# Products of weights for a cross-attention moved from a stage of their own into the recurrent layer's stage of a two-layer decoder kernel

## The reference, cut to what matters

```
x = x + rwkv(ln(x))            # recurrent layer: sigmoid(r) * (decayed sums), then Wo
x = x + xattn(ln(x), context)  # 16 heads, latent keys and values of width 64
x = x + experts8(ln(x)); x = x + gqa(ln(x)); x = x + xattn2(ln(x), context); x = x + experts16(ln(x))
```

```
k, v, r = x @ Wk.T, x @ Wv.T, x @ Wr.T ; w = exp(clip(k)) ; w[:, 0] *= exp(time_first)
num_t = decay * num + w_t * v_t ; den_t = decay * den + w_t        # per channel, over 256 steps
out   = (sigmoid(r) * num / (den + 1e-6)) @ Wo.T

q_big  = rope(einsum(x @ Wq.T, w_kc_q))      # 16 heads x 192
scores = (q_big @ W_qr) . (rope(ctx) @ W_kr) ; attn = softmax(scores)
out    = ((attn @ rope(ctx)) @ w_kc_kv.T) @ Wo.T
```

## Time and profile before

| | |
|---|---|
| time before, median of 3 runs | 1548.04 us |
| lowest and highest of the runs | 1537.82 and 1548.26 us |
| the profiled execution: its own time | 1536.56 us |
| its span (first to last instruction) | 1534.8 us |
| PE busy, share of the span | 1386.6 us, 90% |
| DVE busy | 910.4 us, 59% |
| ACT busy | 641.4 us, 42% |
| POOL busy | 860.8 us, 56% |
| mean granted TensorE clock | 0.947 of full speed |

### The profile page before, as it was taken

The page is one execution under the profiler, slowest core; times in us unless marked ns, Lnnn a source line. Parts: engine busy times, 40 slices in busy tenths (PEclk is TensorE's granted clock), DMA queues, the critical chain, the costliest instruction groups (busy, mean ns, idle before and its releaser), DMA issues.

```text
span 1534.8 us, 21060 instructions
## 1 busy us (share of the span) xinstructions
PE 1386.6 (90%) x7568; PEld 904.0 (59%) x7568; DVE 910.4 (59%) x1615; ACT 641.4 (42%) x1630; POOL 860.8 (56%) x766
## 2 busy tenths in 40 slices
PE   6579997999999999999998567998999988889998
PEld 3466554555555555555557553445777844478887
DVE  6855666566666566666633438996663146646555
ACT  2320112444444444444440324887662247724332
POOL 4415000788888898888890435886442025515554
PEclk9778998899999999999999688998999999979999
DMA  9200111000000000000007320000000041000000
GB/s 263 91 1 14 35 35 35 8 8 8 8 12 8 8 11 7 8 8 11 8 4 251 97 68 9 0 1 1 1 1 25 1 126 63 2 0 1 1 1 28
DMA packets 53375, 48.64 MB, mean 32 GB/s; under 512 B 18048, under 2 KB 49688, under 8 KB 52760
## 3 DMA queue, kind: packets, MB, share of 16 engines
q1 hardware_dynamic: 52504, 45.20, 10.8%
q0 software_dynamic: 768, 2.10, 0.4%
HBM read 34.18 MB, written 4.72 MB: 25 GB/s over the span
## 4 chain that ended last, share of the span: by engine, by line
PE 76%; DVE 10%; ACT 6%; issue 3%; POOL 2%; DMA 1%; SPq 0%; DVEq 0%; POOLq 0%; ACTq 0%
PE PS L435 71%; PE PS L443 4%; ACT s_sc L1120 2%; DVE s_mx L1536 1%; ACT a_m L1086 1%; DVE pm L1357 1%; DVE r_den L1279 1%; DVE PS L1380 1%; POOL a_m L1728 1%; ACT s_pt L944 1%; DVE HN L1229 1%; PE PS L578 1%; POOL a_m L1722 1%; ACT a_sq L1095 1%; ACT QKT L944 1%
## 5 line engine op out<-in xcount | busy, mean ns | idle before, releaser
L1670 POOL TENSOR_TENSOR PWS<-PWS 128x1024 f32<-128x1024 f32 x160 | 379.8, 2373 | 79.8 <-ACT PWS L1026 63.7
L1026 ACT ACTIVATE PWS<-PS 128x512 f32<-128x512 f32 (+1 forms) x416 | 227.8, 595 | 270.0 <-PE PS L435 258.3
L1357 DVE TENSOR_REDUCE pm<-PS 128x2 f32<-128x1024 f32 x192 | 227.4, 1221 | 86.9 <-PE PS L435 86.3
L435 PE MATMUL PS<-PWS,KVR 128*64 128x256 f32 (+1 forms) x1664 | 207.4, 387 | 0.0
L435 PE MATMUL PS<-QALL,KH 128*128 128x512 f32 (+1 forms) x416 | 187.9, 452 | 1.5 <-ACT PWS L1026 1.5
L435 PE MATMUL PS<-QM,KL 68*128 68x512 f32 (+1 forms) x416 | 166.6, 400 | 0.0
L1743 POOL TENSOR_SCALAR s_sc<-s_sc,s_ri 128x128 f32<-128x128 f32 (+1 forms) x256 | 103.9, 425 | 104.0 <-DVE s_ri L1543 104.0
L435 PEld LDWEIGHTS PS<-PWS,KVR 128*64 128x64 f32 (+1 forms) x1664 | 109.8, 137 | 86.4 <-issue 34.7
L1120 ACT ACTIVATE s_sc<-PS,s_nb 128x128 f32<-128x128 f32 (+1 forms) x256 | 104.4, 427 | 58.6 <-DVE s_nb L1539 58.6
L435 PEld LDWEIGHTS PS<-QALL,KH 128*128 128x128 f32 (+1 forms) x416 | 77.7, 187 | 73.0 <-issue 35.6
L1536 DVE TENSOR_REDUCE s_mx<-PS 128x2 f32<-128x512 f32 (+2 forms) x112 | 65.7, 611 | 52.8 <-PE PS L435 52.8
(11 more groups left out here) (279 smaller groups left out, 2854.5 us busy)
## 6 DMA issues: line engine op xcount, KB each, us to landing
QALL<-qlo SPq DMA_DIRECT2D x32, 128.0 KB, 2.4
QM<-QALL SPq DMA_DIRECT2D x64, 64.0 KB, 2.0
f_w<-in_L_ffn_w_dram SPq DMA_DIRECT2D x2, 2048.0 KB
a_nat<-in_L_attn_w_qkv_dram SPq DMA_DIRECT2D x1, 3072.0 KB, 21.5
x_wq<-in_L_xattn_Wq_dram SPq DMA_DIRECT2D x1, 2048.0 KB, 9.3
x_wo<-in_L_xattn_Wo_dram SPq DMA_DIRECT2D x2, 1024.0 KB, 6.7
a_wo<-in_L_attn_w_o_dram SPq DMA_DIRECT2D x1, 2048.0 KB, 21.1
m_wd<-in_L_ffn_Wd_dram SPq DMA_DIRECT2D x1, 2048.0 KB, 8.3
```

The source lines that it names most:

```text
L435: return nc.tensor.matmul(o, a, b, start=start, stop=stop, **kw)
L1026: nc.scalar.activation(PW[c][0:rows, j * HALF:(j + 1) * HALF], PS[0:rows, k % 2 * 512:(k % 2 + 1) * 512], ACT.Exp).then_inc(p_ready, 1)
L1357: ins = V.tensor_reduce(pm[u % 2][:, :, i // 3, i % 3], src, AX, ALU.max)
L1670: G.tensor_tensor(ACC[:, :], PW[0][:, :] if i == 0 else ACC[:, :], PW[i + 1][:, :], ALU.add).then_inc(acc_step, 1)
```

## The change

The work of stage 1 is put into stage 0, between W1 and the wait for `rw_ready`; `ended(eng, 0)` goes, and the later barriers and SP's waits on them count one less. So that this can be done:

- ACT and POOL wait for a new semaphore `scans_done` before they write buffers that lie where the scans' inputs were. DVE gives it after the last scan, on a memset of 128 x 1.
- Buffers move: WqrS to 40960 (over r_decay), x_woT to 145152 (over x_wq), W2 to 104480 (over x_wo0 and r_nat), and WkrT becomes WkrP at 161664 (over x_wqr).
- ACT empties "xwo" and "w2" in place of DVE: the eight "w2" jobs with one copy of 128 x 512 each.
- WkrP holds for each pair of heads three blocks of 64 columns, of which the middle one is zero. With it the two half-height products have 128 moving columns rather than 64 and write the zero quarters themselves. The memset of W2 goes; POOL sets the middle blocks of WkrP (64 x 512) instead.
- POOL makes both strided copies of 64 x 1536 for WqrS.
- `split(0)` on POOL waits for the last "w1" job.

```diff
-        WqrS = at("WqrS", 12288, [D, H * QW])
-        WkrT = at("WkrT", 24576, [D, H * D])
-        x_woT = at("x_woT", 28672, [P, H, C])
+        WqrS = at("WqrS", 40960, [D, H * QW])
+        WkrP = at("WkrP", 161664, [D, PAIRS, 3, D])
+        x_woT = at("x_woT", 145152, [P, H, C])
-        W2 = at("W2", 112672, [P, PAIRS, 2, 256])
+        W2 = at("W2", 104480, [P, PAIRS, 2, 256])
...
             eng.drain().then_inc(phase_ended, 1)
-            eng.wait_ge(phase_ended, 4 * (n + 1))
+            eng.wait_ge(phase_ended, 4 * n)
...                                                     # PE, after the 16 "w1" jobs
-            pe.wait_ge(rw_ready, KC)
-            for t in range(NT):
-                out_product(("ro", t), [(r_num[:, ct, t * P:(t + 1) * P], r_wt[:, 3, ct, :]) for ct in range(KC)])
-            turn_x(1)
-            ended(pe, 0)
             pe.wait_ge(xattn_loaded, 16 * 4)
             for g in range(6):
                 turn(("wqr", g), "act", ...)
             for g in range(2):
                 turn(("wkr", g), "act", ...)
             for g in range(8):
-                turn(("xwo", g), "dve", ...)
+                turn(("xwo", g), "act", ...)
...                                                     # the 4 "u" jobs, unchanged
             pe.wait_ge(*banks.emptied(("wkr", 1)))
             pe.wait_ge(wqr_shift, 2)
+            pe.wait_ge(wkr_padded, 1)
             for p in range(PAIRS):
-                ps = begin(("w2", p), "dve")
+                ps = begin(("w2", p), "act")
                 for c, w in enumerate((WqrT, WqrS)):
-                    A = WkrT[:, 2 * p * D:(2 * p + 1) * D]
-                    A2 = WkrT[:, (2 * p + 1) * D:(2 * p + 2) * D]
+                    A = WkrP[:, p, :, :].rearrange("r k i -> r (k i)")
                     o, g = 256 * c, 3 * p * P
-                    mm(ps[:, o:o + 64], w[:, g:g + P], A)
-                    mm(ps[0:64, o + 64:o + 128], w[:, g + P:g + P + 64], A)
-                    mm(ps[64:128, o + 128:o + 192], w[:, g + P + 64:g + 2 * P], A2)
-                    last = mm(ps[:, o + 192:o + 256], w[:, g + 2 * P:g + 3 * P], A2)
+                    mm(ps[:, o:o + 64], w[:, g:g + P], A[:, 0:64])
+                    mm(ps[0:64, o + 64:o + 192], w[:, g + P:g + P + 64], A[:, 0:128])
+                    mm(ps[64:128, o + 64:o + 192], w[:, g + P + 64:g + 2 * P], A[:, 64:192])
+                    last = mm(ps[:, o + 192:o + 256], w[:, g + 2 * P:g + 3 * P], A[:, 128:192])
                 last.then_inc(filled, 1)
+            pe.wait_ge(rw_ready, KC)
+            for t in range(NT):
+                out_product(("ro", t), ...)
+            turn_x(1)
             ended(pe, 1)
...                                                     # ACT, after its 16 "w1" copies
+            act.wait_ge(scans_done, 1)
+            ...                                         # copies: 6 wqr, 2 wkr, 8 xwo, 4 u, 8 w2
             for g in range(2):
                 deviations(1, g)
...
-            nc.scalar.activation(*wqr_half(1), ACT.Copy).then_inc(wqr_shift, 1)
...                                                     # DVE
+                if ct == KC - 1:
+                    V.memset(pool_tick[:, 0:1], 0.0).then_inc(scans_done, 1)
...
-            for g in range(8):
-                copy_out(("xwo", g), x_woT[:, 2 * g:2 * g + 2, :])
-            V.tensor_copy(*wqr_half(0)).then_inc(wqr_shift, 1)
-            ...                                         # and four copies for each of 8 "w2" jobs
...                                                     # POOL, after kv_roped
-            ended(pool, 0)
-            G.memset(W2[:, :, :, :], 0.0).then_inc(w2_cleared, 1)
+            pool.wait_ge(scans_done, 1)
+            pool.wait_ge(*banks.emptied(("wqr", 5)))
+            for i in range(2):
+                G.tensor_copy(*wqr_half(i)).then_inc(wqr_shift, 1)
+            G.memset(WkrP[:, :, 1, :], 0.0).then_inc(wkr_padded, 1)
...
+            pool.wait_ge(*banks.emptied(("w1", H - 1)))
             split(0)
             ended(pool, 1)
```

More of the change, by code:

```diff
@@ L317, in decoder @@
         kv_roped = sem("kv_roped")
-        w2_cleared = sem("folded_weights_cleared")
+        wkr_padded = sem("key_weights_padded")
+        scans_done = sem("decayed_sums_ready")
         wqr_shift = sem("wqr_shifted")
@@ L515, in _ @@
             for g in range(8):
-                turn(("xwo", g), "dve", [x_wo[ot][:, h * P:(h + 1) * P] for h in (2 * g, 2 * g + 1) for ot in range(KC)])
+                turn(("xwo", g), "act", [x_wo[ot][:, h * P:(h + 1) * P] for h in (2 * g, 2 * g + 1) for ot in range(KC)])
             pe.wait_ge(kckv_loaded, 16)
@@ L527, in _ @@
             pe.wait_ge(wqr_shift, 2)
+            pe.wait_ge(wkr_padded, 1)
             for p in range(PAIRS):
-                ps = begin(("w2", p), "dve")
+                ps = begin(("w2", p), "act")
                 for c, w in enumerate((WqrT, WqrS)):
-                    A = WkrT[:, 2 * p * D:(2 * p + 1) * D]
-                    A2 = WkrT[:, (2 * p + 1) * D:(2 * p + 2) * D]
+                    A = WkrP[:, p, :, :].rearrange("r k i -> r (k i)")
                     o, g = 256 * c, 3 * p * P
-                    mm(ps[:, o:o + 64], w[:, g:g + P], A)
-                    mm(ps[0:64, o + 64:o + 128], w[:, g + P:g + P + 64], A)
-                    mm(ps[64:128, o + 128:o + 192], w[:, g + P + 64:g + 2 * P], A2)
-                    last = mm(ps[:, o + 192:o + 256], w[:, g + 2 * P:g + 3 * P], A2)
+                    mm(ps[:, o:o + 64], w[:, g:g + P], A[:, 0:64])
+                    mm(ps[0:64, o + 64:o + 192], w[:, g + P:g + P + 64], A[:, 0:128])
+                    mm(ps[64:128, o + 64:o + 192], w[:, g + P + 64:g + 2 * P], A[:, 64:192])
+                    last = mm(ps[:, o + 192:o + 256], w[:, g + 2 * P:g + 3 * P], A[:, 128:192])
                 last.then_inc(filled, 1)
+            pe.wait_ge(rw_ready, KC)
+            for t in range(NT):
+                out_product(("ro", t), [(r_num[:, ct, t * P:(t + 1) * P], r_wt[:, 3, ct, :]) for ct in range(KC)])
+            turn_x(1)
             ended(pe, 1)
@@ L982, in _ @@
                          lambda ps: ps[:, 0:KC * QW].rearrange("p (k q) -> p k q", k=KC))
+            act.wait_ge(scans_done, 1)
+            for g in range(6):
+                copy_out(("wqr", g), WqrT[:, g * HALF:(g + 1) * HALF], lambda ps: ps[0:D, :])
+            for g in range(2):
+                copy_out(("wkr", g), WkrP[:, 4 * g:4 * g + 4, 0:3:2, :],
+                         lambda ps: ps[0:D, :].rearrange("r (p s i) -> r p s i", p=4, s=2))
+            for g in range(8):
+                copy_out(("xwo", g), x_woT[:, 2 * g:2 * g + 2, :])
+            for g in range(4):
+                copy_out(("u", g), U[:, 2 * g:2 * g + 2, :])
+            for p in range(PAIRS):
+                copy_out(("w2", p), W2[:, p, :, :])
             for g in range(2):
@@ L1291, in _ @@
                     V.tensor_tensor(z_HTl[:, g, kc, :], ps, z_HTh[:, g, kc, :].bitcast(F32), ALU.subtract).then_inc(emptied["dve"], 1)
-            ended(dve, 0)
-            for g in range(8):
-                copy_out(("xwo", g), x_woT[:, 2 * g:2 * g + 2, :])
-            dve.wait_ge(*banks.emptied(("wqr", 5)))
-            V.tensor_copy(*wqr_half(0)).then_inc(wqr_shift, 1)
[L1299 to L1307, removed]
             ended(dve, 1)
@@ L1821, in _ @@
                 sp.wait_ge(q_moved[s], 32 * PAIRS)
-            sp.wait_ge(phase_ended, 4 * 3)
+            sp.wait_ge(phase_ended, 4 * 2)
             for u in range(UNITS):
@@ L1829, in _ @@
                                  QALL[h * D:(h + 1) * D, p, b, h, :].bitcast(F32)).then_inc(qh_moved[u % 2], 16)
-            sp.wait_ge(phase_ended, 4 * 4)
+            sp.wait_ge(phase_ended, 4 * 3)
             sp.dma_start(g_nat[:, :], L0_ffn_gate_weight).then_inc(moe0_loaded, 16)
@@ L1837, in _ @@
             sp.dma_start(a_wo[:, :, :], L1_attn_w_o.rearrange("(o p) k -> p o k", p=P)).then_inc(gqa_loaded, 16)
-            sp.wait_ge(phase_ended, 4 * 5)
+            sp.wait_ge(phase_ended, 4 * 4)
             sp.dma_start(a_cos[:, :, :], cos1_c).then_inc(gqa_bcast, 16)
@@ L1852, in _ @@
                              f_y[:, e % 3, :].rearrange("p (i c) -> p i c", i=2)).then_inc(res_sent[e % 3], 16)
-            sp.wait_ge(phase_ended, 4 * 6)
+            sp.wait_ge(phase_ended, 4 * 5)
             sp.dma_start(s_mask[:, :], mask_c).then_inc(masks_loaded, 16)
@@ L1861, in _ @@
             sp.dma_start(y_hm[:, :], hmask_c).then_inc(lat_loaded, 16)
-            sp.wait_ge(phase_ended, 4 * 8)
+            sp.wait_ge(phase_ended, 4 * 7)
             sp.dma_start(m_rw[:, :], L1_ffn_router_w).then_inc(moe1_loaded, 16)
@@ L1875, in _ @@
             sp.dma_start(m_wd[:, E1:E1X, :], L1_ffn_Sd[0].rearrange("(s i) c -> i s c", i=P)).then_inc(moe1_loaded, 16)
-            sp.wait_ge(phase_ended, 4 * 10)
+            sp.wait_ge(phase_ended, 4 * 9)
             for t in range(NT):
```

## The result

| | before | after |
|---|---|---|
| median of the runs (4 each) | 1548.15 us | 1526.03 us |
| lowest to highest | 1537.82 to 1549.62 us | 1524.66 to 1528.07 us |
| ratio | | 0.9872, 95% interval 0.9827 to 0.9917 |
| profiled execution, its span | 1536.56, 1534.8 us | 1528.07, 1525.9 us |
| first z product | 121.34 us | 104.39 us |

The changed kernel is faster by 1.3%. The medians are 22.1 us apart and the two profiled spans 8.9; the stretch that was changed became 17.0 us shorter (121.34 - 104.39).

A forecast was written before the change was run, and what follows sets the result against it. PE idled from 50.7 to 68.71 us behind DVE's reciprocals, then stage 1 took 34.8 us on PE. Moving it gave 26, taken as 25: 1511.6 from the profiled execution, 1523 from the median; predicted 1516, range 1508 to 1534.

The forecast's parts named there:

- rival 2: PE from U on: half clock all the way through U, W2 and output products; 9 us less; chance 0.06.
- the low level: Whole time: the profiled execution of before, 1536.6 us, next to the lowest run and 11.5 us under the median.
- Turns and U: Before W2: ACT's 16 bank copies, 8.8 us together, set U's start at 60.4; U takes 3.6 us, ending at 64.0.
- POOL: Ahead of W2: two strided copies at 1.6 us each and a 0.4 us memset, done at 58.5, hidden; cost 0.
- W2's columns: W2's half-height products: 128 moving columns for 64 add 0.11 us a group at full clock, 0.21 at half.
- W2's clock: W2 on PE: full clock held through 16 groups at 0.95, 15.2 us, ending at 79.2; 26.5 us at half.
- rival 1: W2: clock falls as before, 22.3 us, and output products start at half clock; 17 us less; chance 0.22.
- Output products to the barrier: After W2: 17.8 us before, 1.9 less at full clock, so 15.9 us, ending at 95.1.
- rival 3: Turns before U: they do not hold the clock, U starts 1 us later; about 23 us less; chance 0.06.
- Nothing after the start of the z products is altered: 1413.5 us that I leave as they are: From the first z product, 121.34 us before, to the end: 1413.5 us taken as unchanged.
- the sum of 1511.6: Whole time against the profiled execution: 1536.6 - 25 us.

The follow-up runs named there:

- pool_more: The changed kernel with POOL making each of its two 64x1536 copies four times over; first z product at 115.0 us, 10.6 us later.
- batched: The changed kernel with the four full-height products of both groups before the four half-height ones in each W2 job; median 1524.57 us, ratio 0.9837 to before.
- rowpair: The changed kernel with heads 8 to 15 in partitions 64 to 127, two pairs of heads at once in W2; median 1510.0 us, ratio 0.9764 to before.
- w2_twice: The kernel `rowpair` with each W2 product made twice into the same place; W2 from 63.3 to 76.4 us, first z product at 92.6 us.
- cols64: The changed kernel with 64 moving columns in W2's half-height products and its zero quarters left unset; 1528.0 us in one run.
- gap2: The changed kernel with W2 ordered as in `batched` and the last two W2 jobs between the halves of `turn_x(1)`; 1519.63 us, ratio 0.9829 to before.
- w2_late: The changed kernel with the W2 jobs behind the output products and the turns of the normalised x; 1538.5 us in one run.

## Why the prediction was right, and where it was not

- **Direction and size**: 1516 was predicted, within 1508 to 1534, and 1526.03 measured. The median fell by 22.1 us where 25 was forecast. That the two lie so close is in part luck: up to z only 17.0 us came of the 25, and the rest is from the later part, of which the prediction said that it stays. Nor does the range tell one mechanism from another: it was said to leave out rival 2, but from the low level rival 2 gives 1536.6 - 9 = 1527.6, inside it.
- **Turns and U**: U at 60.4 forecast, 58.83 measured. The copies took 0.50 us each (4.01 for eight), not 0.56. ACT was free at 58.74 and x_kckv landed at 58.37: two limits nearly level, of which I had named one. U took 3.6 us.
- **POOL**: 1.43 us a copy against 1.6, done at 57.8, hidden. `pool_more` bears the slack out.
- **W2's columns**: 0.11 and 0.21 us a group forecast, 0.10 and 0.22 measured.
- **W2's clock, the step that failed**: "16 * 0.95 = 15.2 us at full". The clock fell as in the kernel before, and W2 took 23.4 us. This is rival 1, whose 17 us less to z is what came (17.0), with parts that were off and cancelled: U began 1.6 us earlier than forecast, W2 took 1.1 more than the 22.3 of that rival, and the output products 0.7 more than 17.8. I gave it 0.22, although the row of before was the only evidence and spoke for it. The argument against it, more columns in nearly the same time, carried nothing: `batched` raised the density further and the clock fell sooner. What held it in `rowpair` and `w2_twice` was a second set of products in the other half of the rows.
- **Output products to the barrier**: 18.5 us (85.88 to 104.39), where 17.8 belongs to a start at half clock.
- **Turns and the clock**: rival 3 fell. 50.20 to 57.30 holds turns and is at 1.00, which again goes against what the Trainium skill says in "TensorE: Matmul & The Clock Gate", Part 4: PE-mode transpose, that turns do not bring the full clock.
- **"Nothing after the start of the z products is altered: 1413.5 us that I leave as they are"**: the instructions are the same, the time is not. It was 1413.5 to 1423.9 in three executions of one kernel. Against the profiled execution the sum of 1511.6 missed 1528.07 by 16.5 us: 8 in the early part (z forecast at 96.3) and 8 in the later one. Against the median, 1523 missed by 3, although the early part was off by the same 8 us: the later part made up for most of it.
- Of the 22.1 us between the medians, 17.0 to 18.2 are shown in the early part. The other 4 to 5 belong to executions without a trace; that they are shorter falls of the clock is argued only.

## What to carry to other kernels

Moving work into an engine's hole gives at most the smaller of hole and work, less what the moved work loses or plus what it gains in its new place (W2 took 19.4 us before and 23.4 after): read which row says at what clock it ran, and price it so until another row says otherwise. When small products with K = 64 follow each other on one half of the rows, look for a second set to put into the other half before looking at their order; it took W2 from 23.4 to 6.6 us. Take the trace of before more than once when the runs show two levels, and cut it at the first instruction that the change leaves alone: the second part tells how large a difference is no difference.

## What the runs showed of the hardware that was not expected

- TensorE, busy without a stop, went from 2.4 to 1.2 GHz within 2.8 to 5.7 us of products with K = 64 on one half of the rows, in every form that had them at full clock at the start (the kernel before, the changed one, `cols64`, `batched`, `gap2`). With the same products in both halves, two at a time, it stayed at 2.4 GHz for 13.1 us.
- Once down, such products do not bring it back: 26.7 us at 0.50 in `w2_late`.
- In the attention, where PE stands 1.4 us between two groups of contexts, the clock sometimes falls for 6.8 or 13.4 us (3.0 and 6.3 us of time) and sometimes does not, in the same kernel.
- A POOL copy of 64 x 1536 took 1.43 us and one of 128 x 768 0.80 (`rowpair`), with the same number of elements in all: in these two it goes by the elements in a partition, not by the number of partitions.
